# Local attention and feed-forward in one software pipeline: feed-forward steps in other slots, shifted inputs out of PSUM and by ScalarE

## The reference

```python
def attn_layer(x, Wqkv, qs, ksc, Wo):
    q, k, v = heads(x @ Wqkv)                 # 16 heads of 64
    q, k = l2norm(q) * qs, l2norm(k) * ksc
    q, k = rotary(q), rotary(k)               # scaled up for q, down for k
    out = local_attention(q, k, v)            # windows of 32 that see one window back
    return merge(out) @ Wo
def ffn_layer(x, g, bln, W1, b1, W2, b2):
    xn = layernorm(x) * g + bln
    a, gate = split(xn @ W1 + b1)             # 341 each
    return a * gelu(gate) @ W2 + b2
for i in range(6):
    x = attn_layer(shift_tokens(x)) + x
    x = ffn_layer(shift_tokens(x)) + x
```

## Time and profile before

| | us |
|---|---|
| median of 2 runs | 2680.75 (2680.68 to 2680.82) |
| the profiled execution's own time | 2675.91 |
| its span in the trace | 2674.1 |
| local attention, first to last scores | 99 to 2121 |

### The profile page before, as it was taken

The page is one execution under the profiler, slowest core; times in us unless marked ns, Lnnn a source line. Parts: engine busy times, 40 slices in busy tenths (PEclk is TensorE's granted clock), DMA queues, the critical chain, the costliest instruction groups (busy, mean ns, idle before and its releaser), DMA issues. The chain is left out here.

```text
span 2674.1 us, 62735 instructions
## 1 busy us (share of the span) xinstructions
PE 2425.9 (91%) x24940; PEld 1267.4 (47%) x24940; DVE 1953.1 (73%) x2595; ACT 1795.8 (67%) x2593; POOL 1082.0 (40%) x461
## 2 busy tenths in 40 slices
PE   7899999999999999999999999999999977777778
PEld 2355554555554555555555555555555522222355
DVE  5677777778677877778677877787678658999542
ACT  4677766777677766777667776777667656545533
POOL 0344444444444444444444444444444303556130
PEclk8999999999999999999999999999999989999889
DMA  0100000000000000000000000000000010000001
GB/s 21 53 2 2 2 25 10 10 2 2 14 22 10 2 2 14 16 15 2 2 14 14 16 4 2 14 14 10 10 2 2 2 37 0 0 0 0 18 17 47
DMA packets 16016, 29.85 MB, mean 11 GB/s; under 512 B 3616, under 2 KB 6064, under 8 KB 15664
## 3 DMA queue, kind: packets, MB, share of 16 engines
q1 hardware_dynamic: 15760, 25.78, 3.1%
HBM read 24.73 MB, written 1.05 MB: 10 GB/s over the span
## 5 line engine op out<-in xcount | busy, mean ns | idle before, releaser
L708 POOL TENSOR_TENSOR f_rot<-f_raw,f_tabc 128x1024 f32<-128x1024 f32 x192 | 452.7, 2358 | 727.3 <-ACT f_raw L606 332.4
L712 POOL TENSOR_TENSOR f_rot<-f_rot,f_shuf 128x1024 f32<-128x1024 f32 x192 | 453.0, 2359 | 481.0 <-DVE f_shuf L749 481.0
L606 ACT ACTIVATE f_raw<-f_ps 128x1024 f32<-128x1024 f32 x192 | 196.5, 1023 | 364.4 <-PE f_ps L430 364.4
L477 PEld LDWEIGHTS f_ps<-f_ptz,f_v 64*64 64x64 f32 x6144 | 260.1, 133 | 95.0 <-issue 94.9
L775 DVE TENSOR_REDUCE f_sum<-f_ps 128x8 f32<-128x512 f32 x192 | 131.8, 686 | 217.2 <-ACT f_ps L662 217.1
L477 PE MATMUL f_ps<-f_ptz,f_v 64*64 64x96 f32 (+1 forms) x6144 | 286.4, 243 | 1.5 <-ACT f_ptz L627 1.4
L746 DVE STREAM_SHUFFLE f_shuf<-f_raw 128x1024 f32<-128x1024 f32 x192 | 254.8, 1327 | 0.0
L756 DVE SCALAR_TENSOR_TENSOR f_qk<-f_rn,f_rot 128x1024 f32<-128x1024 f32 x192 | 233.4, 1215 | 23.9 <-POOL f_rot L712 23.9
L429 PE MATMUL f_ps<-f_xs,f_wq 128*128 128x512 f32 x384 | 226.3, 673 | 24.2 <-DVE f_xs L727 20.8
L749 DVE TENSOR_TENSOR f_shuf<-f_shuf,f_tabs 128x1024 f32<-128x1024 f32 x192 | 236.7, 1233 | 8.7
L456 PE MATMUL f_ps<-f_qk 64*32 64x64 f32 x12288 | 198.3, 220 | 34.6 <-issue 34.6
(11 more groups left out here) (267 smaller groups left out, 3971.7 us busy)
## 6 DMA issues: line engine op xcount, KB each, us to landing
e_w<-in_e_w SPq DMA_DIRECT2D x16, 256.0 KB, 2.9
f_wq<-in_f_wq SPq DMA_DIRECT2D x12, 256.0 KB, 2.8
f_wk<-in_f_wk SPq DMA_DIRECT2D x12, 256.0 KB, 3.4
f_wv<-in_f_wv SPq DMA_DIRECT2D x12, 256.0 KB, 3.5
f_wo<-in_f_wo SPq DMA_DIRECT2D x6, 512.0 KB, 3.4
f_w<-in_f_w SPq DMA_DIRECT2D x6, 341.0 KB, 3.0
s_dx<-in_k_pick SPq DMA_DIRECT2D x1, 1536.0 KB, 9.0
f_w<-in_f_w SPq DMA_DIRECT2D x6, 192.0 KB, 3.3
```

The costliest lines, as they stand in the source:

```text
L477: mm = pe.matmul(view(ps, 7 * CH + 64 * p, [1, n], p0=64 * h, rows=64), v[64 * h:64 * h + 64, p * CH + 64 * j:p * CH + 64 * j + 64], ptz[6 ...
L708: pool.tensor_tensor(view(rot, 0, [S, 4], [1, S]), view(raw, 0, [S, 4], [1, S]), view(tab_c, 0, [S, 2], [0, 2], [1, S]), ALU.mult).then_in ...
L712: pool.tensor_tensor(rot[:, :], rot[:, :], shuf[:, :], ALU.add).then_inc(sem["rot"], 1)
```

## The change

The feed-forward steps of unit k go to other places of the pipeline. On TensorE: `mean` in slot 3 right behind scores, needing y1 too; `variance` in slot 3; the first gate in slot 4, in bank 3; the other two gates in slot 5, where mix goes ahead of project and project of the pair 7 waits for the gelus; the third hidden part in slot 7 right behind scores; and norms become the last step of every slot, behind variance, gate, hidden part and `w2_mm`. ScalarE follows: square and root in slot 3 (the square behind the exponential), scale and bias and the first gelu in slot 4, the others at the start of slot 5. On ScalarE too, in slot 5, `shift_in` forms the next unit's shifted input xs with three copies. On VectorE xs2 is formed by three additions of y and bank 3 (`centre_in`), ahead of y1; centring follows the maximum and subtraction in slot 3, the scaling goes ahead of the rotation in slot 4, `hidden(k, 1)` behind the rotation in slot 6, and `hidden(k, 2)` behind the softmax in slot 7.

```diff
-        GBANK = (2, 0, 1)
+        GBANK = (3, 0, 1)
...
@@ -407,10 +407,6 @@
-                if q == 7:
-                    need(pe, sem["ln2"], i)
-                if q == 0:
-                    need(pe, sem["gelu"], i * 3 - 6 + 1 + G0)
...
-                if j == 0:
-                    need(pe, sem["gelu"], i * 3 - 6 + 3 + G0)
+                if j == 7:
+                    need(pe, sem["gelu"], i * 3 + G0)
                 need(pe, sem["ln"], i * 8 + j)
...
             def mean(i):
                 need(pe, sem["xs2"], i + 1)
+                need(pe, sem["y1"], i + 1)
                 pe.matmul(bank(3), con.ones[:, :], xs2[:, :], start=True, stop=True).then_inc(sem["mean"], 1)
 
-            def variance(i, run):
+            def variance(i):
                 need(pe, sem["sq2"], i + 1)
-                if run:
-                    need(pe, sem["v"], i * 8 + 8 + 7)
-                pe.matmul(bank(2), con.ones[:, :], sq2[:, :], start=True, stop=True).then_inc(sem["var"], 1)
+                pe.matmul(bank(3), con.ones[:, :], sq2[:, :], start=True, stop=True).then_inc(sem["var"], 1)
 
...
             def hid_mm(i, f):
                 if f:
                     need(pe, sem["hid"], i * 3 + f + H0_)
+                else:
+                    need(pe, sem["gelu"], i * 3 + 1 + G0)
...
@@ -534,11 +531,15 @@
                     scores(i, j)
                 if before and j == 2:
                     wo_part(k, 6, 8)
-                if before and j == 6:
-                    need(pe, sem["ln"], i * 8 + 8 if run else 0)
+                if before and j == 3:
+                    mean(k)
+                if before and j == 5:
+                    need(pe, sem["ln"], i * 8 + 7 if run else 0)
                     gate_mm(k, 1)
                     gate_mm(k, 2)
-                if j == 6 and had2:
+                if before and j == 7:
+                    hid_mm(k, 2)
+                if j == 5 and had2:
                     mix(u2, b2)
                 if has:
                     if j == 7:
@@ -546,29 +547,24 @@
                     project(u, a)
                     if j != 7:
                         values(u, a)
-                if j != 6 and had2:
+                if j != 5 and had2:
                     mix(u2, b2)
                 if before and j < 2:
                     wo_part(k, 3 * j, 3 * j + 3)
-                if before and j == 3:
-                    mean(k)
                 if before and j == 6:
                     hid_mm(k, 1)
-                if before and j == 7:
-                    hid_mm(k, 2)
                 if had1:
                     turn(u1, b1)
-                if has:
-                    norms(u, a)
+                if before and j == 3:
+                    variance(k)
                 if before and j == 4:
-                    variance(k, run)
+                    gate_mm(k, 0)
                 if before and j == 5:
-                    if run:
-                        need(pe, sem["v"], i * 8 + 8)
-                    gate_mm(k, 0)
                     hid_mm(k, 0)
                 if before and j == 7:
                     w2_mm(k)
+                if has:
+                    norms(u, a)
...
@@ -633,6 +629,18 @@
                     need(act, sem["wo_mm"], i)
                 act.activation(o[:, UNIT * j:UNIT * j + UNIT], bank(7), ACT.Copy).then_inc(sem["o"], 1)
 
+            def shift_in(i):
+
+                need(act, sem["a_mm"], i * 8)
+                need(act, sem["v_mm"], i * 8)
+                need(act, sem["y2"], i + 1 - NU + Y0)
+                unit = i % NU
+                act.activation(xs[0:64, :], y[0:64, bass.ds(unit * UNIT, UNIT)], ACT.Copy)
+                for b in range(2):
+                    ins = act.activation(xs[64:128, b * S + 1:b * S + S], y[64:128, bass.ds(unit * UNIT + b * S, S - 1)],
+                                         ACT.Copy)
+                ins.then_inc(sem["xs"], 1)
...
@@ -646,43 +654,45 @@
                 had2, u2, b2 = (run, i, j - 2) if j >= 2 else (before, k, j + 6)
                 if j == 0:
                     nc.scalar.preload_act_table_set(ACT_SET)
-                if before and j == 6:
+                if before and j == 5:
                     gelu(k, 1)
                     gelu(k, 2)
                     nc.scalar.preload_act_table_set(ACT_SET)
                 if has:
                     raw_copy(u, a)
-                if before and j == 4:
-                    need(act, sem["cen"], k + 1)
-                    act.activation(sq2[:, :], cen[:, :], ACT.Square).then_inc(sem["sq2"], 1)
-                if has and j == 5:
-                    value_copy(u, a)
                 if run:
                     need(act, sem["shift"], i * 8 + j + 1)
                     act.activation(view(ps, 4 * CH, [CH, 2], [64, 4], [1, 64]), view(s[j % 2], 0, [64, 2], [128, 4], [1, 64]),
                                    ACT.Exp, scale=8.0).then_inc(sem["exp"], 1)
-                if has and j != 5:
+                if before and j == 3:
+                    need(act, sem["cen"], k + 1)
+                    act.activation(sq2[:, :], cen[:, :], ACT.Square).then_inc(sem["sq2"], 1)
+                if has:
                     value_copy(u, a)
-                if before and j == 5:
+                if j == 5 and more:
+                    shift_in(i + 1)
+                if had2:
+                    out_copy(u2, b2)
+                if before and j == 4:
                     need(act, sem["scaled"], k + 1)
                     act.activation(xn[:, :], xn[:, :], ACT.Identity, scale=fcol[:, 0:1], bias=fcol[:, 1:2]).then_inc(sem["xn"], 1)
-                if had2:
-                    out_copy(u2, b2)
                 if had1:
                     spread(u1, b1)
                 if has:
                     inverse_norm(u, a)
-                if before and j == 4:
+                if before and j == 3:
                     need(act, sem["var"], k + 1)
-                    act.activation(sq2[:, :], bank(2), ACT.Ln, bias=con.eps).then_inc(sem["ln2"], 1)
+                    act.activation(sq2[:, :], bank(3), ACT.Ln, bias=con.eps).then_inc(sem["ln2"], 1)
                     need(act, sem["ln2"], k + 1)
                     act.activation(sq2[:, :], sq2[:, :], ACT.Exp, scale=-0.5).then_inc(sem["rs2"], 1)
-                if before and j == 5:
+                if before and j == 4:
                     gelu(k, 0)
...
             n1.scalar(act, n1_banks, con.eps)
             act.wait_ge(sem["const"], n_const)
+            act.wait_ge(n1.out, n1.n + NCH)
+            act.wait_ge(sem["zero"], 1)
...
         @block.vector
         def _(dve):
-            def shift_in(to, unit, done):
-
-                dve.tensor_scalar(to[0:64, :], y[0:64, bass.ds(unit * UNIT, UNIT)], 1.0, None, ALU.mult)
+            def centre_in(k):
+
+                need(dve, sem["wo_mm"], k + 1)
+                dve.tensor_tensor(xs2[0:64, :], y[0:64, bass.ds((k % NU) * UNIT, UNIT)], view(ps, 3 * CH, [1, UNIT], rows=64),
+                                  ALU.add)
                 for b in range(2):
-                    mm = dve.tensor_scalar(to[64:128, b * S + 1:b * S + S], y[64:128, bass.ds(unit * UNIT + b * S, S - 1)],
-                                           1.0, None, ALU.mult)
-                mm.then_inc(done, 1)
+                    mm = dve.tensor_tensor(xs2[64:128, b * S + 1:b * S + S],
+                                           y[64:128, bass.ds((k % NU) * UNIT + b * S, S - 1)],
+                                           view(ps, 3 * CH + b * S, [1, S - 1], p0=64, rows=64), ALU.add)
+                mm.then_inc(sem["xs2"], 1)
...
@@ -796,45 +809,38 @@
                 ycol = y[:, bass.ds((k % NU) * UNIT, UNIT)] if before else None
                 if run:
                     soft_a(i, j)
-                if before and j == 6:
-                    hidden(k, 0)
-                if before and j == 7:
-                    hidden(k, 2)
-                if next1:
-                    normalise(u1, a1)
-                if j == 6 and more:
-                    tables(i + 1)
-                if before and j == 6:
-                    hidden(k, 1)
-                if run:
-                    soft_b(i, j)
-                if has:
-                    rotate(u, a)
-                if before and j == 2:
-                    need(dve, sem["wo_mm"], k + 1)
-                    dve.tensor_tensor(ycol, ycol, bank(3), ALU.add).then_inc(sem["y1"], 1)
-                    need(dve, sem["y1"], k + 1)
-                    shift_in(xs2, k % NU, sem["xs2"])
                 if before and j == 3:
                     need(dve, sem["gelu"], k * 3 + G0)
                     dve.tensor_scalar(fcol[:, :], cols[:, bass.ds((k // NU) * 13 + 4, 9)], 1.0, None, ALU.mult).then_inc(sem["fcol"], 1)
                     need(dve, sem["mean"], k + 1)
                     need(dve, sem["xs2"], k + 1)
```

(24 more changed lines are left out.)

## The result

| | before | after |
|---|---|---|
| median, us | 2680.75 | 2968.91 (2967.63 to 2970.19, 2 runs) |
| ratio, 95% interval | | 1.1075 (1.1027 to 1.1123) |
| span of the profiled execution, us | 2674.1 | 2968.4 |

The changed kernel is 10.8% slower. The forecast was 3050 us in a range of 2935 to 3140: direction and range hold, the point is 81 us too high.

The account below looks back on a forecast made before the run. TensorE was taken as the bound, waits in its stream paid in full. To 2675.9 us came 279 of net waits and 90 of clock, 3045; with the median 4.8 us above the profiled execution, 3050 us, range 2935 to 3140.

Parts of the forecast that it names:

- The eight waits: Slots 3 to 7: steps moved ahead on TensorE wait for inputs not yet ready, 14.35 us a unit in sum.
- (1): Slot 3: `mean`, right behind scores, waits for VectorE's y1, ready at +8.89 while scores end at +5.9; 3.2 us.
- (3): Slot 4: the first gate, moved before norms, waits for its scaled input xn from VectorE; 3.5 us.
- (6): Slot 6: the next unit's projection waits for ScalarE's line 615 of slot 5, queued behind its copies; 1.2 us.
- (8): Slot 7: `w2_mm`, moved before norms, waits for `hidden(k, 2)`, now behind the softmax; 3.4 us.
- The clock behind the long waits: Slots 3, 4, 7: TensorE drops to 1.2 GHz behind each long wait; 1.3 us each, 3.9 a unit, 90 us.
- rival E: Slots 5 to 7: clock falls behind the shorter waits too, twice more a unit; 60 us, 3110 us; chance 0.06.
- Slots 0 to 2 keep their order and their time.: Slots 0 to 2: order unchanged and TensorE saturated, so time unchanged; only about 0.3 us off at the loop's start.
- A: Whole unit: waits come as worked out, but the clock stays up or its loss lies beside them; 2960 us; chance 0.16.
- B: Half of the waits: VectorE or ScalarE run further ahead, two of three long ones shrink away; 2838 us; chance 0.08.
- C: No new wait is met, inputs being ready when TensorE comes; 2630 us; chance 0.05 for it or a part.
- D: Slot 4: GpSimd's line 708 still runs and stops VectorE's line 827; 29 us more, 3079 us; chance 0.05.

Follow-up runs that it names:

- a_mean: Changed kernel with one part undone: mean back behind mix in slot 3; 2876.2 us.
- a_gate0: Changed kernel with one part undone: in slot 4 norms again ahead of the first gate; 2898.0 us.
- a_w2: Changed kernel with one part undone: `w2_mm` again behind norms in slot 7, `hidden(k, 2)` ahead of normalise; 2908.1 us.
- a_three: Changed kernel with mean behind mix, first gate and `w2_mm` behind norms, and `hidden(k, 2)` ahead of normalise, all at once; 2748.6 us.
- a_fill3: Changed kernel with three unneeded matmuls of 512 columns added on TensorE ahead of mean in slot 3; 2931.6 us.
- b_hint: Kernel before with a hint to the loop's branch at the top of every pass; 2591.9 us, 0.9686 of before.
- a_w2_hint: Changed kernel with `w2_mm` again behind norms, `hidden(k, 2)` ahead of normalise, and the loop's branch hinted; 2855.5 us.
- b_centre: Kernel before with only xs2 formed by three additions out of PSUM, all steps in their old slots; 2646.4 us, 0.9894.

## Why the prediction was right, point by point

**TensorE is the bound, and a wait in its stream is paid in full.** Right: 23 waits a step, and each of the three long ones, undone, gave back its wait (the first gate's all but 1.26 us, as expected of its place) and its half clock (a_mean, a_gate0, a_w2), additively (a_three).

**The eight waits.** Per unit, from the rows above (totals over 23; for 514 the 0.86 of slot 7, for 445 the 0.29 of slot 6):

| | forecast, us | measured, us |
|---|---|---|
| (1) mean for y1 | 3.2 | 3.18 |
| (2) variance for the square | 0.5 | 0.20 |
| (3) first gate for xn | 3.5 | 2.98 |
| (4) project for the gelus | 1.1 | 0.89 |
| (5) scores of slot 6 for p | 0.45 | 0.29 |
| (6) next unit's project for the inverse norm | 1.2 | 1.32 |
| (7) hidden part | 1.0 | 0.86 |
| (8) w2_mm | 3.4 | 2.97 |
| sum | 14.35 | 12.7 |

The method holds: offsets from the start of V, taken from one slot of before, come back in others. The 0.2 us from a release to TensorE's start was too much: in (1) it is 1090.03 to 1090.17, 0.14, and in (3) and (8) of the same unit 0.05. That the records end a matmul some 0.17 us after the next could start makes the printed idle time smaller than the loss: line 461 begins at 1106.29 in slot 4 and would have been followed 0.49 us later, at 1106.78, not at 1106.95 where the 2.98 us begin.

**The clock behind the long waits.** Right in kind, small in size: forecast 1.3 us for each of three, 3.9. The slots at 0.89, 0.88 and 0.90 are worth 0.11 x 14.92, 0.12 x 13.70 and 0.10 x 17.33, 1.6 to 1.7 us each, 5.0 us in a unit that has all three, and a_fill3 gives 1.6 us for one in the total. The clock fell behind (1) in all 21 passes, behind (3) in 18 and behind (8) in 20, which makes 4.7 us a unit in the mean. So my discount for work that lies before another wait was not there: `mean`, P, norms and `w2_mm` all lie on the chain. Behind the waits of 0.9 to 1.3 us in slots 5 and 6 (rival E) it fell once in the 21 passes of after, in slot 6; but with the first gate undone it fell in slot 6 in 7 of 21, behind the same 1.31 us. So E was nearly absent here and not impossible.

**"Slots 0 to 2 keep their order and their time."** This is the step that failed. Their order they kept, but slot 0 took 10.69 us in the mean in place of 14.16: 3.47 us in each of 21 passes, 73 us. The forecast had taken off 0.3 us a unit for it, 7 us, so 66 of the 81 us between 3050 and 2969 are this step. I had priced the gap at the start of each pass (1.65 us and about 1.8 us of clock) as a cost of the loop that stays. It depends on what TensorE does near the end of the pass: held at `w2_mm`, it has its instructions 1.8 us earlier against the scores (after), without that wait it hasn't (a_w2), and with the hint the gap goes in every pass (b_hint, a_w2_hint). Of the remaining 15 us, 6 are the two profiled executions' places among their runs.

For slots 3 to 7 the forecast was 14.35 us of waits and 3.9 of clock, less 1.93 for the gaps of the kernel before, 16.3 us a unit; measured are 16.2. That is closer than the terms deserve, and luck: 1.65 us a unit too much in waits stands against 0.8 too little in clock and the share of each stall that the idle time doesn't show. Together, 23 x 16.2 less 73 is 300 us, and the two spans lie 294 apart.

**The slots.** Forecast with the fall of the clock 14.8, 13.4 and 17.0 us for slots 3, 4 and 7; measured 14.91, 13.42 and 17.22. Stretches at half clock were to come four times a unit; they come three times, as the one in slot 0 is gone.

**The rivals.** A (2960 us) comes nearest in its number and is wrong in its mechanism: the clock does fall in slots 3, 4 and 7. B and C fall with the table. D: the multiply of line 827 (829 in after) was not stopped by GpSimd; it took 0.68 to 0.69 us in all 24 units, and in the unit shown GpSimd's line 718 had ended 0.54 us before it began. What shifting the input cost ScalarE was put at 1.1 us; its rows are 0.62 and 0.72 for the three copies, 1.34, within the bounds.

## What to carry to other kernels

Where one engine is saturated, put into its stream right behind a result's producer the work that needs nothing new, and take a step's price as chain minus the work ahead of it, from offsets against an event that recurs. An edit that leaves a stretch's order alone can still change its time: ask of each gap that looks fixed what hides or uncovers it, above all at a loop's branch. A single change can hold a part that gains (here 30 us) inside a whole that loses 288; only the parts alone show it.

## What was not expected of the hardware

The gap behind a loop's branch, 1.65 us on TensorE in each of 21 passes, with the half clock behind it, cost 2676.5 - 2591.9 = 85 us or 3.2% of the kernel; a semaphore wait of 3 us with five matmuls between it and the branch hides it in nearly every pass (1.4 us left in all), the hint in every pass, at the price of one gap behind the loop. In this place the clock fell in 3 of 21 passes behind gaps of 1.35 us in the mean (a_w2), in 8 behind 1.30 (a_three), in 14 behind 1.63 (b_centre) and in 20 behind 1.65 (before): shorter gaps mostly leave it alone, but no single length divides the two. And useless matmuls in a wait paid for themselves: 37 us faster for 72 matmuls more.
